# Attention with row maxima formed ahead of the scores: the lead of the maxima cut from four key tiles to two

## The chip, the cores and the metric

The kernel runs on one core of a Trainium2 chip. The metric is the device time of one execution in microseconds (us), the median of several runs. Times inside an execution come from the trace of one profiled execution and count from the start of its span.

## The reference

Inputs are x of shape (2, 2048, 256), three 256x256 projections with biases, and the weights of a gated feed-forward layer. There are 16 heads of width 16, so 32 (batch, head) pairs, called heads 0 to 31 below.

```python
q = hidden_states @ Wq + bq          # k, v alike
q = q * cos_pos + _rotate_half_interleaved(q) * sin_pos   # k alike
scores = jnp.einsum('bhqd,bhkd->bhqk', q, k) / jnp.sqrt(jnp.asarray(HD, hidden_states.dtype))
probs = jax.nn.softmax(scores, axis=-1)
ctx = jnp.einsum('bhqk,bhkd->bhqd', probs, v)
...
x = _layernorm(x + attention(x), axis=-1)
x = _layernorm(x + ffn(x), axis=-1)  # token shift, sigmoid gate, squared relu
```

All of it is float32. The softmax runs over 2048 keys for each of 2048 queries of each head.

## The kernel before

Each head has a period of 16 key tiles (`TILES`). In a tile, PE (TensorE) forms four score matrices of 128 keys x 512 queries (L712), ACT (ScalarE) takes their exponential (L893), and PE multiplies the probabilities of the tile before with the values (L664). A slot is half a tile: two score matmuls and half of such a product. The score matmul has 50 rows: 48 of queries and keys, and two that subtract each query's maximum. So the maxima of a head must stand in its stack of queries (`q_stack`) before its first score.

They are formed ahead by a second stream. A unit is a tile of 128 queries against half of the keys: two matmuls into one of two PSUM tiles `ring_ps` (L645), then one maximum over 128x1024 on DVE (VectorE, L1225). A head has 32 units (`MAX_UNITS`). The maxima matmuls use the half of PE's rows that the scores of the running head leave free. `period_ops(h)` writes the order out by hand: in tile `kt` of head h the units 2*kt + `EARLY` and the one after, of head h+1, or, from 32 on, of head h+2. `EARLY` = 2 * `LEAD`, so with `LEAD` = 4 the last four tiles of a period work on units 0 to 7 of the head after next, which are read from a copy of its stack on the free side (`load_copy`, whose queries reach to `COPY_Q`).

Once unit 31 of head h+1 is read, DVE folds the unit maxima into `neg_max` (L1198, "cut"), POOL (GpSimd) splits it in a high and a low part (`neg_cuts`), DVE turns them (`neg_turned`, L1232, "negs", in tile `NEG_CYCLE`), and SP (SyncE's queue) moves them in two transfers that follow each other:

```python
sp.dma_start(neg_d[h % 2], neg_turned[:, h % 2]).then_inc(neg_out, DMA)      # L461
sp.wait_ge(neg_out, (h + 1) * DMA)
sp.dma_start(dst..., neg_d[h % 2]...).then_inc(neg_in[h % STACKS], DMA)      # L464
```

PE waits for the second at the start of the period, ahead of the first score of the head (`pe.wait_ge(neg_in[...])` in `period`). The last product of the head before stands behind that wait, in tile 0.

Ahead of head 0 there is an opening: 40 units (32 of head 0, eight of head 1) in pairs, behind each pair one or two of 32 projection steps (L609, L622), as `BEHIND_PAIR` says. The transfer for head 0 is asked for behind unit 33 (`OPENING`). In the period of head 30 there is no head after next, so its last four tiles have no units. Head 31's period has none at all, and the feed-forward part follows.

Of the kernel before, what the change touches and what calls it, by code (L numbers as in the profile page):

```python
# [22 lines left out]
BLOCKS = SEQ // TOK  # L23
# [26 lines left out]
PV_CREDIT = 2  # L50
RING_CREDIT = 2
MAX_UNITS = 2 * TILES
LEAD = 4
EARLY = 2 * LEAD
COPY_Q = EARLY // 2 * P
FIRST_COPY = SIDES
TWIN = STACKS - 1
TWIN_FROM = EARLY
NEG_CYCLE = TILES - LEAD
NEG_LOADS = 1  # L60
CTX_BUFS = 2
# [66 lines left out]

OPENING = [("max", 0, u) for u in range(MAX_UNITS)] + [("cut", 0, 0)]
OPENING += [("max", 1, 0), ("max", 1, 1), ("negs", 0, 0)] + [("max", 1, u) for u in range(2, EARLY)]  # L130
BEHIND_PAIR = (2, 1, 2, 1, 2) * ((MAX_UNITS + EARLY) // 10)


def ring_len(ops):
# [29 lines left out]
def build(nc, x_tok, x_blk, w_first, w_qk, b_qk, w_v, b_v, w_rkv, mu, tables, out):  # L164
# [7 lines left out]
    with ExitStack() as ctx:  # L172
# [201 lines left out]
        def stack_rows(h, first, count):  # L374

            side = h % SIDES * SIDE_ROWS
            return slice(side + first, side + first + count)

        def slot_of(h):
            return h // SIDES % (STACKS // SIDES)  # L380
# [199 lines left out]
        def _(pe):  # L580
# [46 lines left out]
            def maximum(k, h, unit):  # L627
# [10 lines left out]
                if (h, unit) == (0, TILES):  # L638
                    pe.wait_ge(late_queries, LATE_QUERIES * DMA)
                if (h, unit) == (0, TWIN_FROM):  # L640
                    pe.wait_ge(twin_in, 3 * PARTS * DMA)
                for c in range(2):
                    if h == 0 and unit >= TWIN_FROM and c:
                        rows, slot = stack_rows(TWIN, 0, ROWS), slot_of(TWIN)
# [110 lines left out]
            for k, op in enumerate(op for op in OPENING if op[0] == "max"):  # L755
                for _ in ring_ops([op], k):
                    pass
                if k % 2:
                    for _ in range(BEHIND_PAIR[k // 2]):
                        project(n)  # L760
# [743 lines left out]
```

## Time and profile before

| | |
|---|---|
| median of 3 runs | 1468.39 us (1467.81 to 1470.98) |
| the profiled execution, its own time | 1470.37 us |
| its span in the trace | 1468.5 us |
| granted clock of PE | 0.999 of full speed |
| busy: PE, DVE, ACT, POOL | 1444.7, 1377.8, 1193.6, 311.5 us |
| first score of heads 16 and 17 | 742.28 and 782.02 us, so a period of 39.75 us |

The execution's own time is 1.9 us over the span, for what lies around it. Busy shares are averages over an opening (to 105 us), 32 periods (to 1385 us) and a last part. What a wait costs is read in its own stretch.

### The profile page before, as it was taken

To read this page: it belongs to the slowest core of one execution; us is meant where nothing else is said; L and a number is where in the kernel's file an instruction comes from. 1 tells how busy PE (TensorE), PEld (TensorE's weight loads), DVE (VectorE), ACT (ScalarE), POOL (GpSimd) and SP (SyncE) were. 2 spreads that over 40 slices of the span, in tenths; PEclk is the share of its full clock that TensorE was granted. 3 is DMA by queue.
4 is the path that set the end of the run, shared out by engine and by line. 5 is a ranking of instruction groups with operands and counts; after the bars stand their busy time and mean duration, and the time that the engine had idled before them with its cause. 6 is when DMAs were issued, how large, how long until landed. Compare 5 with 4: busy or idle time off the path is not lost.

```text
span 1468.5 us, 31675 instructions
## 1 busy us (share of the span) xinstructions
PE 1444.7 (98%) x13108; PEld 604.7 (41%) x13108; DVE 1377.8 (94%) x1457; ACT 1193.6 (81%) x2185; POOL 311.5 (21%) x279
## 2 busy tenths in 40 slices
PE   7999999999999999999999999999999999999998
PEld 6673333333333333333333333333333333333475
DVE  6669999999999999999999999999999999997396
ACT  3338888888888888888888888888888888888745
POOL 5250321032102210032103210241002000001175
PEclk9999999999999999999999999999999999999999
DMA  5845222232223211222223222321112323200153
GB/s 161 241 148 189 41 37 37 37 94 37 37 37 95 36 27 25 79 40 37 36 37 95 37 37 37 95 37 28 23 26 36 51 36 52 37 2 8 24 119 111
DMA packets 72816, 88.20 MB, mean 60 GB/s; under 512 B 48560, under 2 KB 58416, under 8 KB 66464
## 3 DMA queue, kind: packets, MB, share of 16 engines
q1 hardware_dynamic: 72112, 85.39, 27.6%
q8 instruction: 103, 1.69, 0.5%
q10 hardware_dynamic: 560, 0.79, 0.2%
q14 instruction: 41, 0.34, 0.1%
HBM read 29.50 MB, written 14.16 MB: 30 GB/s over the span
## 4 chain that ended last, share of the span: by engine, by line
PE 95%; DVE 2%; ACT 1%; DMA 1%; issue 0%; POOL 0%; POOLq 0%; DVEq 0%
PE pv_ps L664 39%; PE score_ps L712 32%; PE ring_ps L645 15%; PE score_ps L609 2%; PE ring_ps L684 2%; PE score_ps L794 2%; ACT probs L893 1%; PE pv_ps L778 1%; PE score_ps L778 1%; PE pv_ps L609 1%; DVE tile_max L1225 1%; PE score_ps L622 1%; DVE rope L1161 0%; DVE rope L1157 0%; DMA b_qk_s<-b_qk 0%
## 5 line engine op out<-in xcount | busy, mean ns | idle before, releaser
L1225 DVE TENSOR_REDUCE tile_max<-ring_ps 128x1 f32<-128x1024 f32 x1024 | 1232.4, 1217 | 33.7 <-PE ring_ps L645 25.5
L893 ACT ACTIVATE probs<-score_ps 128x512 f32<-128x512 f32 x2048 | 1108.0, 595 | 170.1 <-PE score_ps L712 129.9
L712 PE MATMUL score_ps<-q_stack,k_stack 50*128 50x512 f32 x2048 | 755.0, 448 | 7.1 <-ACT probs L893 6.9
L645 PE MATMUL ring_ps<-k_stack,q_stack 48*128 48x512 f32 x2048 | 736.5, 444 | 0.8 <-DVE tile_max L1225 0.8
L664 PE MATMUL pv_ps<-probs,v_aug 128*32 128x256 f32 x8192 | 649.0, 391 | 0.0
L712 PEld LDWEIGHTS score_ps<-q_stack,k_stack 50*128 50x128 f32 x2048 | 304.4, 185 | 429.1 <-ACT probs L893 412.2
L664 PEld LDWEIGHTS pv_ps<-probs,v_aug 128*32 128x32 f32 x8192 | 165.9, 108 | 367.4 <-issue 190.0
L645 PEld LDWEIGHTS ring_ps<-k_stack,q_stack 48*128 48x128 f32 x2048 | 301.2, 184 | 9.7 <-issue 5.9
L990 POOL TENSOR_TENSOR neg_cuts<-neg_max,zeros 128x16 fp32r<-128x16 f32 x31 | 6.9, 222 | 491.1 <-DVE neg_max L1198 491.1
L982 POOL TENSOR_TENSOR v_aug<-v_all,b_v_s 128x256 f32<-128x256 f32 x32 | 23.7, 741 | 309.6 <-PE pv_ps L664 252.9
L999 POOL TENSOR_TENSOR ctx_part<-ctx_turn,recip 128x256 f32<-128x256 f32 x32 | 20.1, 627 | 266.8 <-DVE recip L1252 266.8
L1011 POOL TENSOR_TENSOR rope<-rope 128x2048 f32<-128x2048 f32 x14 | 63.8, 4572 | 16.7 <-DMA rope<-qk_raw 16.7
L1247 DVE STREAM_TRANSPOSE ctx_turn<-pv_ps 128x512 f32<-128x512 f32 x32 | 22.6, 706 | 21.9 <-PE pv_ps L664 21.9
L1017 POOL TENSOR_TENSOR rope<-rope 128x2048 f32<-128x2048 f32 x7 | 32.1, 4584 | 0.1
L1032 POOL TENSOR_TENSOR rope<-rope 128x2048 fp32r<-128x2048 f32 x7 | 32.0, 4572 | 0.1
L845 ACT ACTIVATE probs<-score_ps,b_qk_s 128x512 f32<-128x512 f32 x21 | 14.2, 688 | 21.9 <-PE score_ps L609 13.7
L684 PE MATMUL ring_ps<-w_rkv_s,rope 128*32 128x256 f32 (+1 forms) x224 | 31.6, 379 | 0.0
L924 ACT ACTIVATE v_all<-score_ps 128x512 f32<-128x512 f32 x14 | 7.6, 594 | 24.6 <-PE score_ps L794 24.6
L684 PEld LDWEIGHTS ring_ps<-w_rkv_s,rope 128*32 128x32 f32 (+1 forms) x224 | 22.5, 144 | 7.3 <-issue 2.4
L794 PE MATMUL score_ps<-rope,w_rkv_s 128*128 128x512 f32 x56 | 25.3, 594 | 0.0
L1327 DVE SCALAR_TENSOR_TENSOR rope<-rope,mu_s 128x512 f32<-128x512 f32 x32 | 22.4, 758 | 2.3 <-ACT rope L905 2.2
L1004 POOL TENSOR_TENSOR z_s<-z_s,ctx_part 128x256 f32<-128x256 f32 x32 | 23.7, 741 | 2.5
(139 smaller groups left out, 550.2 us busy)
## 6 DMA issues: line engine op xcount, KB each, us to landing
k_stack<-rope SPq DMA_DIRECT2D x61, 256.0 KB, 5.0
k_stack<-rope SPq DMA_DIRECT2D x63, 128.0 KB, 4.7
q_stack<-rope SPq DMA_DIRECT2D x31, 256.0 KB, 4.4
qk_raw<-probs SPq DMA_DIRECT2D x28, 256.0 KB, 4.4
rope<-qk_raw SPq DMA_DIRECT2D x7, 1024.0 KB, 4.8
rope<-qk_raw SPq DMA_DIRECT2D x14, 512.0 KB, 6.6
q_stack<-rope SPq DMA_DIRECT2D x33, 128.0 KB, 4.9
z_s<-x_tok SPq DMA_DIRECT2D x2, 2048.0 KB, 11.7
```

Of the source, the lines that this page charges most:

```text
L609: mm = pe.matmul(bank, w[:, c, :], x[:, c, :], start=term == 0 and c == 0, stop=term == 2 and c == CHUNKS - 1)
L645: mm = pe.matmul(ring_ps[k % 2][:, c * TOK:(c + 1) * TOK], q_stack[rows, slot, qt * P:(qt + 1) * P], k_stack[rows, slot, lo + c * TOK:lo + ...
L664: mm = pe.matmul(pv_ps[j * VCOLS:(j + 1) * VCOLS, t], v_aug[:, h % 2, kt, :], probs[:, kt % 2, j, t], start=kt == 0 and half == 0, stop=kt ...
L684: mm = pe.matmul(r_ps[n][g:g + width, q * DIM:(q + 1) * DIM], mixed[:, n % MIXED_BUFS, 0, c, q * P + g:q * P + g + width], w_rkv_s[:, 0, c ...
L712: mm = pe.matmul(score_ps[n % SCORE_BANKS][:, :], k_stack[rows, slot, kt * P:(kt + 1) * P], queries[:, j], start=True, stop=True)
L778: mm = pe.matmul(value_ps[q // 2][:, q % 2 * DIM:(q % 2 + 1) * DIM], key_act[:, n % 2, c, q * P:(q + 1) * P], w_rkv_s[:, 2, c, :], start=c ...
L794: mm = pe.matmul(o, w_rkv_s[:, 1, c, m * P:(m + 1) * P], mixed[:, n % MIXED_BUFS, 1, c, :], start=c == 0, stop=c == CHUNKS - 1)
L893: act.activation(probs[:, kt % 2, j, :], score_ps[n % SCORE_BANKS][:, :], ACT.Exp, scale=SCALE).then_inc(exps_done, 1)
L1011: pool.tensor_tensor(blocks, blocks, tables_s[:, :, w, :], ALU.mult).then_inc(quad_step, 1)
L1017: pool.tensor_tensor(raw, raw, swapped, ALU.add).then_inc(quad_step, 1)
L1032: pool.tensor_tensor(cuts[:, g % 2, 1, :].bitcast(F32R), raw, cuts[:, g % 2, 0, :], ALU.subtract)\
L1225: dve.reduce_max(tile_max[:, h % 2, unit // 2, unit % 2:unit % 2 + 1], slot[:, :], AX.X)\
```

## The change

`LEAD` goes from 4 to 2, and with it `EARLY` from 8 to 4. The order of a period moves: units 4 to 31 of head h+1 fill tiles 0 to 13, and units 0 to 3 of head h+2 the last two tiles. `cut` moves from the end of tile 11 to the end of tile 13, and `negs` from tile 12 to tile 14 (`NEG_CYCLE` = `TILES` - `LEAD`). The copy of a stack holds 256 queries in place of 512 (`COPY_Q`). `TWIN_FROM` keeps its value of 8. The opening has 36 units, and `BEHIND_PAIR` spreads the same 32 projection steps behind 18 pairs in place of 20. The last four units of head 31, which stood in tiles 10 and 11 of head 30's period, stand in its tiles 12 and 13, and the four fewer of the opening are made up there.

```diff
-LEAD = 4
+LEAD = 2
 EARLY = 2 * LEAD
 COPY_Q = EARLY // 2 * P
 FIRST_COPY = SIDES
 TWIN = STACKS - 1
-TWIN_FROM = EARLY
+TWIN_FROM = BLOCKS * 2
 NEG_CYCLE = TILES - LEAD
...
-BEHIND_PAIR = (2, 1, 2, 1, 2) * ((MAX_UNITS + EARLY) // 10)
+BEHIND_PAIR = (2, 1, 2, 2, 2) * 3 + (2, 2, 1)
```

DVE's order in a period, from the maxima ahead of the fold to the reciprocal of the next period (L1247 turns the product of the finished head in tile 0), before:

```order
L1225 TENSOR_REDUCE tile_max<-ring_ps 128x1 x14
L1198 TENSOR_REDUCE neg_max<-tile_max 128x16
L1225 TENSOR_REDUCE tile_max<-ring_ps 128x1
L1232 STREAM_TRANSPOSE neg_turned<-neg_cuts 128x32
L1225 TENSOR_REDUCE tile_max<-ring_ps 128x1 x8
L1247 STREAM_TRANSPOSE ctx_turn<-pv_ps 128x512
```

And now:

```order
L1225 TENSOR_REDUCE tile_max<-ring_ps 128x1 x18
L1198 TENSOR_REDUCE neg_max<-tile_max 128x16
L1225 TENSOR_REDUCE tile_max<-ring_ps 128x1
L1232 STREAM_TRANSPOSE neg_turned<-neg_cuts 128x32
L1225 TENSOR_REDUCE tile_max<-ring_ps 128x1 x4
L1247 STREAM_TRANSPOSE ctx_turn<-pv_ps 128x512
```

The fold and the turn stand four maxima later; between the turn and the next period's L1247 stand four maxima in place of eight. PE's order at the end of the opening, from its last pair of units to the first score of head 0, before:

```order
L645 MATMUL ring_ps<-k_stack,q_stack 128x512 x4
L622 MATMUL score_ps<-w_high,x_split 128x256 x4
L622 MATMUL score_ps<-w_low,x_split 128x256 x2
L622 MATMUL score_ps<-w_high,x_split 128x256 x4
L622 MATMUL score_ps<-w_low,x_split 128x256 x2
L622 MATMUL score_ps<-w_high,x_split 128x256 x4
L622 MATMUL score_ps<-w_low,x_split 128x256 x2
L622 MATMUL score_ps<-w_high,x_split 128x256 x4
L622 MATMUL score_ps<-w_low,x_split 128x256 x2
L712 MATMUL score_ps<-q_stack,k_stack 128x512
```

And now:

```order
L645 MATMUL ring_ps<-k_stack,q_stack 128x512 x4
L622 MATMUL score_ps<-w_high,x_split 128x256 x4
L622 MATMUL score_ps<-w_low,x_split 128x256 x2
L622 MATMUL score_ps<-w_high,x_split 128x256 x4
L622 MATMUL score_ps<-w_low,x_split 128x256 x2
L712 MATMUL score_ps<-q_stack,k_stack 128x512
```

One projection step stands behind the last pair in place of two, and that pair is now units 34 and 35, not 38 and 39. The orders of ACT and POOL are the same as before, and SP's differs in the size of the copies alone.

## Rows read from the trace of the kernel before

**Rows 1.** Busy time by stretch: from:to, length, engines' busy us, clock, DMA share, GB/s.

```profile
600.00:1000.00 400.00, 397.85 (x3866) 149.49 (x3864) 397.04 (x373) 348.33 (x644) 87.00 (x70) 1.00 0.26 50
```

**Rows 2.** The page, section 5: busy, mean ns | idle before, releaser.

```profile
L1225 DVE TENSOR_REDUCE tile_max<-ring_ps 128x1 f32<-128x1024 f32 x1024 | 1232.4, 1217 | 33.7 <-PE ring_ps L645 25.5
...
L645 PE MATMUL ring_ps<-k_stack,q_stack 48*128 48x512 f32 x2048 | 736.5, 444 | 0.8 <-DVE tile_max L1225 0.8
```

**Rows 3.** Timeline of PE around the start of head 16: start, length, what.

```profile
734.86 0.50 PE L712 MATMUL score_ps<-q_stack,k_stack 50*128 50x512 f32 x1
...
739.80 0.50 PE L712 MATMUL score_ps<-q_stack,k_stack 50*128 50x512 f32 x1
...
741.71 0.64 PE L664 MATMUL pv_ps<-probs,v_aug 128*32 128x256 f32 x8
742.28 0.50 PE L712 MATMUL score_ps<-q_stack,k_stack 50*128 50x512 f32 x1
```

**Rows 4.** Timeline of DVE in the same stretch.

```profile
733.21 0.19 DVE L1198 TENSOR_REDUCE neg_max<-tile_max 128x16 f32<-128x32 f32 x1
...
734.45 0.20 DVE L1232 STREAM_TRANSPOSE neg_turned<-neg_cuts 128x32 f32<-128x32 f32 x1
734.57 9.74 DVE L1225 TENSOR_REDUCE tile_max<-ring_ps 128x1 f32<-128x1024 f32 x8
```

**Rows 5.** Timeline of SP's DMA issues in the same stretch.

```profile
734.68 0.32 SPq L461 DMA_DIRECT2D neg_turned_rows<-neg_turned  x1
736.09 0.67 SPq L464 DMA_DIRECT2D q_stack<-neg_turned_rows  x1
```

**Rows 6.** Busy time by stretch, same place, for its DMA share.

```profile
735.60:735.80 0.20, 0.20 (x8) 0.08 (x8) 0.20 (x2) 0.20 (x1) 0.00 (x0) 1.00 0.22 32
...
738.00:738.20 0.20, 0.20 (x6) 0.15 (x8) 0.19 (x2) 0.20 (x1) 0.00 (x0) 1.00 0.14 21
738.20:738.40 0.20, 0.20 (x8) 0.00 (x0) 0.20 (x1) 0.20 (x1) 0.00 (x0) 1.00 0.00 0
```

**Rows 7.** The same view ahead of head 4.

```profile
261.20:261.40 0.20, 0.20 (x8) 0.00 (x0) 0.20 (x1) 0.20 (x2) 0.00 (x0) 1.00 0.01 1
261.40:261.60 0.20, 0.20 (x6) 0.18 (x4) 0.20 (x1) 0.20 (x1) 0.00 (x0) 1.00 0.00 0
```

**Rows 8.** Timeline of PE at the first score of head 4.

```profile
265.14 0.50 PE L712 MATMUL score_ps<-q_stack,k_stack 50*128 50x512 f32 x1
```

**Rows 9.** Waits of SP's queue: line, releaser: us in total, times, longest.

```profile
SPq L464 <- DMA neg_turned_rows<-neg_turned: 43.0, 32, 3.1
```

**Rows 10.** Timeline of PE in head 30's last tiles, without maxima.

```profile
1336.18 0.74 PE L712 MATMUL score_ps<-q_stack,k_stack 50*128 50x512 f32 x2
...
1337.41 0.73 PE L712 MATMUL score_ps<-q_stack,k_stack 50*128 50x512 f32 x2
```

**Rows 11.** Timeline of PE at the end of the opening.

```profile
101.04 1.20 PE L645 MATMUL ring_ps<-k_stack,q_stack 48*128 48x512 f32 x4
102.17 0.74 PE L622 MATMUL score_ps<-w_high,x_split 128*128 128x256 f32 x4
...
105.46 0.47 PE L712 MATMUL score_ps<-q_stack,k_stack 50*128 50x512 f32 x1 [0.20 <-ACTq L881]
```

**Rows 12.** Timeline of DVE at the end of the opening.

```profile
95.95 0.21 DVE L1232 STREAM_TRANSPOSE neg_turned<-neg_cuts 128x32 f32<-128x32 f32 x1 [1.39 <-POOL neg_cuts L992]
...
99.08 2.35 DVE L1225 TENSOR_REDUCE tile_max<-ring_ps 128x1 f32<-128x1024 f32 x2 [0.68 <-PE ring_ps L645]
```

**Rows 13.** Timeline of SP at the end of the opening.

```profile
98.27 0.76 SPq L464 DMA_DIRECT2D q_stack<-neg_turned_rows  x1
```

**Rows 14.** Busy time by stretch at the end of the execution.

```profile
1461.00:1463.00 2.00, 1.31 (x7) 0.80 (x5) 1.90 (x8) 1.36 (x3) 1.61 (x3) 1.00 0.00 0
1463.00:1465.00 2.00, 0.00 (x0) 0.00 (x0) 1.85 (x8) 0.89 (x2) 1.70 (x4) 1.00 0.79 262
1465.00:1468.50 3.50, 0.00 (x0) 0.00 (x0) 0.64 (x2) 0.20 (x1) 0.45 (x1) 0.55 0.45 150
```

## The prediction

> **What bounds the kernel now.** I read first a long stretch of the periods by engine. In the 400 us from 600 to 1000, PE is busy 397.85 us and DVE 397.04 us, at full clock [rows 1]: both stand within 1% of full. The idle times say which of them leads. DVE idled 33.7 us in the whole execution, most of it for PE's maxima matmuls, while those matmuls waited 0.8 us for DVE [rows 2]. So PE sets the pace and DVE runs right behind it. PE's timeline shows the pace: scores start at 734.86 and at 739.80, four slots apart [rows 3], 4.94 us or 1.235 us a slot. Thirty-two slots make 39.5 us of a period of 39.75 us. At the end of head 30, where no maxima are formed, a slot takes 1337.41 - 1336.18 = 1.23 us [rows 10], the same: the maxima matmuls cost PE no time beside the scores. What matters for the change is then the one thing that PE needs at a head's start and that it does not need to wait for today: the negated maxima.
>
> **The way of the negated maxima today.** For head 16, DVE folds at 733.21 and turns from 734.45 to 734.65 [rows 4]; SP stores at 734.68 and starts the reload at 736.09 [rows 5], 1.41 us later. The store's last packets fall before 735.8 [rows 6], some 0.4 us ahead of the issue that waits for them, which I take as the time from the last packet to the semaphore. The reload has no recorded landing, but the DMA share shows it: packets until 738.2, none after [rows 6]. With 0.4 us more it lands at 738.6, that is 2.5 us after its issue and 3.95 us after the turn. PE's first score of head 16 starts at 742.28 [rows 3]. The slack is 3.68 us. For head 4 the last packets fall right behind 261.2 [rows 7], the landing is at 261.6, the first score at 265.14 [rows 8]: 3.54 us of slack.
>
> **The change part by part.**
>
> *Fold and turn four units later.* DVE takes one unit for each slot of PE, with no backlog (the idle times above), so four units are four slots: 4.94 us [rows 3]. POOL's cut stands between fold and turn, and its distance to both is unchanged. Everything behind the turn moves with it: two transfers, and SP has nothing else to issue between them. PE's need does not move. The wait at the head's start is 4.94 - 3.68 = 1.26 us by head 16 and 4.94 - 3.54 = 1.40 us by head 4. I take the mean, 1.33 us, for 31 heads (1 to 31): 41.2 us.
>
> *Slower stores.* SP waited 43.0 us in 32 times for the store, up to 3.1 us [rows 9]. Head 16's wait was 736.09 - 735.00 = 1.09 us [rows 5], and 32 of these are 34.9 us. So 8.1 us lie over that, in a few heads. In the opening it was 98.27 - 96.51 less 1.09 = 0.67 us (the turn ends at 96.16 [rows 12], and the store is issued for 0.32 us right behind it). The other 7.4 us come straight on PE's waits: every head waits now, so no slack takes them up. + 7.4 us.
>
> *Starting again.* A score overlaps the end of the product ahead of it by 0.07 us (741.71 + 0.64 against 742.28 [rows 3]). After a wait it does not: 31 x 0.07 = 2.2 us. Nothing is won back behind the wait: the last product of the head before stands behind it in PE's order, so the period's first tile runs as today, late as a whole. ACT and DVE only idle: both take their work from PE.
>
> *The opening.* Four units fewer. Two units take PE 102.17 - 101.04 = 1.13 us [rows 11], and there nothing runs beside them, so PE would come to the first score 2.26 us earlier, at 103.2. But head 0's transfer is asked for behind unit 33, and behind that unit's pair stand now three projection steps and one pair instead of six and three. A step takes (105.3 - 102.17) / 2 = 1.56 us, with 105.3 for the end of the last (the score at 105.46 idled 0.2 before it [rows 11]). Unit pair 32 and 33 then starts 3 x 1.56 + 1.13 + 1.13 = 6.9 us ahead of 103.2, at 96.3. DVE is done with a pair 99.08 + 2.35 - 98.3 = 3.1 us after PE begins it (PE begins that pair one step and one pair ahead of 101.04, at 98.3 [rows 11, 12]), so at 99.4; the turn adds 0.2. The two transfers took 98.27 - 96.16 = 2.1 us to the reload's issue [rows 12, 13], and 2.5 us more as above: the first score can start at 104.2 in place of 105.46. The opening gives 1.2 us. Its bounds are 2.3 us (no wait) and nothing.
>
> *At no cost.* The four units that the opening gives up end in tiles 12 and 13 of head 30, where a slot lasts as long with them as without. The smaller copies leave SP and the DMAs less to do. The loads of the stacks keep their places and have most of a period. In head 30 DVE's first work for the feed-forward part moves 5 us back behind the turn; it serves head 31's later tiles, and PE comes to these later too.
>
> The sum: 41.2 + 7.4 + 2.2 - 1.2 = 49.6 us. On the profiled execution's 1470.37 us this gives 1520.0 us, on its span 1518.1 us. That execution lies 2 us over the median of the runs, so the time I predict for the median is 1468.39 + 49.6 = **1518.0 us**.
>
> *The bounds.* The reload's time is the one unseen price. From below, it could take what the store takes from issue to landing, 1.41 us, and 0.35 us more for its longer issue (0.67 against 0.32 [rows 5]): 1.76 in place of 2.5 us. That is 0.74 us less a head, 23 us in all, 1495 us. From above, every store could wait 43.0 / 32 = 1.34 us and some heads up to 3.1 us; if all took 0.7 us more than head 16's, as the worst heads do in part, that would be 22 us less the 7.4 counted: 1533 us.
>
> **The rivals.**
>
> *The wait brings PE's clock down.* At the end of the execution PE stops at 1462.3, keeps the full clock to 1465, and shows 0.55 of it after [rows 14]. So some 3 us of idling are followed by the half clock. The waits that I expect are 1.3 us in most heads, and near 3 us in one or two. If the clock fell at each head and stayed at half for a few slots, each such slot would take up to 1.23 us more; two of them a head are 31 x 2.46 = 76 us more, about 1594 us. It decides from waits near 3 us on. Against it: 1.3 us stays well under the one pause for which a row shows a fall. I give it 4 in 100. The Trainium skill ("TensorE: Matmul & The Clock Gate", "HAM oscillation — how this bites in real kernels") tells of a matmul loop that pauses for a DMA at each step and starts cold every time. By that rule the half clock would come back at each head; whether a pause of 1.3 us is enough, no row here shows.
>
> *The stores are slow everywhere.* Something at tiles 14 and 15 makes both transfers longer, such as the slow stores of some heads [rows 9]. Then 0.7 to 1 us more a head: 1535 to 1545 us. For it: it happens in some heads, for a reason that I cannot read. Against it: the DMA share is close to nothing around these transfers [rows 6, 7] and stays so two tiles later, since SP issues the next loads only after a head's last score. 9 in 100.
>
> *The transfers are hidden (no slower).* The turn would end at 734.65 + 4.94 = 739.6, 2.69 us ahead of the first score. If both transfers landed within these 2.69 us, no head would wait, and the opening alone would count: 1468.39 - 2.3 = 1466.1 us. That is the point from which it decides. Against it stand the 3.95 us above, and the store alone, which takes 1.44 us of them from the turn to the reload's issue; the reload would have to land 1.25 us after its issue, and its packets still flow 1.9 us after it [rows 6]. 3 in 100.
>
> **How the numbers follow.** My forecast has 84 in 100, the clock 4, slow stores 9, the hidden transfers 3. The range from 1495 to 1540 us takes in the bounds of the reload and most of the slow stores. A difference under 0.2% (3 us) is what a measurement of this kernel can't tell from no change. The forecast and two of the rivals lie far over it; the third lies within it, 2 us faster. So slower 0.96, same 0.03, faster 0.01.
>
> **What the profile after would show.** Right: a period of about 41.1 us in place of 39.75; PE's first score of each head idle ahead of it for 1.2 to 1.5 us, with the reload's DMA as the releaser, and about 3 us at the worst head; DVE's idle time up by some 45 us, ACT's too; slots inside a period still 1.235 us; first score of head 0 near 104.2; clock at 1.00 in every period. Wrong: slots longer right behind a wait (the clock), reloads issued 2 us behind the turn in all heads (slow stores), or first scores with no idle time (hidden). The prediction falls most easily with the reload's landing, which I read from packets and an added 0.4 us.

## The result

The changed kernel takes 1563.99 us (median of 4 runs, 1553.87 to 1594.11), the kernel before 1468.45 us (1467.81 to 1470.98): a ratio of 1.0624, 95% interval 1.0581 to 1.0667. That is slower, as forecast, but by 95.5 us in place of 49.6, and above the range of 1495 to 1540 us. Times scatter over 40 us where before they lay within 3. Ratios, here and in the table below, leave out runs that lie over 1.5% above the fastest of their kernel (here the one of 1594.11 us), so they can be lower than the quotient of the medians. The profiled execution is the longest of them (span 1592.3 us), so its rows are read for the mechanism, and the sizes are set against all runs.

The page of the kernel after: busy time, the clock granted to PE in 40 slices of the span (tenths; 9 is 90% or more), and the two groups that answer to [rows 2] and to the scores.

```profile
PE 1522.9 (96%) x13108; PEld 625.7 (39%) x13108; DVE 1378.8 (87%) x1457; ACT 1193.6 (75%) x2185; POOL 311.6 (20%) x279
...
PEclk9999999968978667699999999999999999999999
...
L1225 DVE TENSOR_REDUCE tile_max<-ring_ps 128x1 f32<-128x1024 f32 x1024 | 1235.4, 1218 | 154.2 <-PE ring_ps L645 147.2
...
L712 PE MATMUL score_ps<-q_stack,k_stack 50*128 50x512 f32 x2048 | 795.2, 470 | 52.6 <-DMA q_stack<-neg_turned_rows 46.4
```

The clock stood at 9 in every slice before:

```profile
PEclk9999999999999999999999999999999999999999
```

It falls here in eight slices, all in the first half. DVE's idle time before its maxima grew from 33.7 to 154.2 us, by 120 us in place of the 45 us foreseen, and the scores idle 46.4 us for the reload of the negated maxima, which did not show before. The waits of PE name it too (us in total, times, longest):

```profile
PE score_ps L712 <- DMA q_stack<-neg_turned_rows: 46.4, 31, 3.1
```

For an ordinary head, 16, the timelines of DVE, SP and PE answer to [rows 3] to [rows 5]:

```profile
839.83 0.20 DVE L1232 STREAM_TRANSPOSE neg_turned<-neg_cuts 128x32 f32<-128x32 f32 x1
...
844.83 1.23 DVE L1225 TENSOR_REDUCE tile_max<-ring_ps 128x1 f32<-128x1024 f32 x1 [1.32 <-PE ring_ps L645]
```

```profile
840.05 0.32 SPq L461 DMA_DIRECT2D neg_turned_rows<-neg_turned  x1
841.46 0.67 SPq L464 DMA_DIRECT2D q_stack<-neg_turned_rows  x1
```

```profile
842.14 0.64 PE L664 MATMUL pv_ps<-probs,v_aug 128*32 128x256 f32 x8
843.99 0.50 PE L712 MATMUL score_ps<-q_stack,k_stack 50*128 50x512 f32 x1 [1.21 <-DMA q_stack<-neg_turned_rows]
```

The turn ends at 840.03, the reload is issued at 841.46, and PE idles 1.21 us from the end of the product to the first score. This is the prediction's step, to 0.1 us. DVE idles as long. The first score of head 0 starts at 102.40, where the prediction had 104.2. Here is head 5, with a slow store (SP, then PE):

```profile
307.75 0.32 SPq L461 DMA_DIRECT2D neg_turned_rows<-neg_turned  x1
310.76 0.66 SPq L464 DMA_DIRECT2D q_stack<-neg_turned_rows  x1
```

```profile
309.83 0.64 PE L664 MATMUL pv_ps<-probs,v_aug 128*32 128x256 f32 x8
313.54 0.77 PE L712 MATMUL score_ps<-q_stack,k_stack 50*128 50x512 f32 x1 [3.07 <-DMA q_stack<-neg_turned_rows]
```

The store took 3.01 us to the reload's issue, PE idled 3.07 us, and its first score took 0.77 us in place of 0.50. Busy time by period, from head 4 to head 8 and for head 16 (from:to, length, PE, PEld, DVE, ACT, POOL, granted clock, DMA share, GB/s):

```profile
270.50:313.50 43.00, 39.73 (x384) 14.95 (x384) 39.47 (x36) 34.53 (x64) 2.55 (x5) 1.00 0.21 34
313.50:369.80 56.30, 54.18 (x384) 18.84 (x384) 39.97 (x36) 34.65 (x64) 11.54 (x7) 0.70 0.23 58
369.80:417.20 47.40, 45.35 (x384) 16.48 (x384) 39.73 (x36) 34.65 (x64) 8.93 (x7) 0.86 0.18 28
417.20:458.90 41.70, 39.69 (x385) 14.89 (x385) 39.47 (x36) 34.65 (x64) 7.08 (x6) 1.00 0.20 32
458.90:512.30 53.40, 51.19 (x384) 17.97 (x385) 39.96 (x36) 34.64 (x64) 2.53 (x5) 0.74 0.16 25
844.00:885.20 41.20, 39.69 (x385) 14.91 (x385) 39.46 (x36) 34.64 (x64) 2.55 (x5) 1.00 0.22 34
```

The same 384 matmuls take 56.3 us with a mean clock of 0.70 in head 5 and 41.2 us at full clock in head 16.

### The profile page after: what moved, and what is told of

The parts are those of the page before. It is cut to its first block, busy times and chain, and to the rows that moved or that the text cites. A ratio compares the mean times of both kernels' runs of the same rounds, so it can differ in the third digit from the quotient of the medians.

```text
span 1592.3 us, 31675 instructions
## 1 busy us (share of the span) xinstructions
PE 1522.9 (96%) x13108; PEld 625.7 (39%) x13108; DVE 1378.8 (87%) x1457; ACT 1193.6 (75%) x2185; POOL 311.6 (20%) x279
## 4 chain that ended last, share of the span: by engine, by line
DVE 55%; PE 30%; DMA 9%; issue 4%; ACT 0%; POOL 0%; POOLq 0%; DVEq 0%; ACTq 0%
DVE tile_max L1225 53%; PE score_ps L712 11%; PE pv_ps L664 9%; DMA q_stack<-neg_turned_rows 5%; DMA neg_turned_rows<-neg_turned 3%; PE ring_ps L645 2%; PE score_ps L609 2%; PE ring_ps L684 2%; PE score_ps L794 2%; DVE ctx_turn L1247 1%; PE pv_ps L778 1%; PE score_ps L778 1%; DMA qk_raw<-probs 1%; PE pv_ps L609 0%; DVE neg_turned L1232 0%
## 5 line engine op out<-in xcount | busy, mean ns | idle before, releaser
L1225 DVE TENSOR_REDUCE tile_max<-ring_ps 128x1 f32<-128x1024 f32 x1024 | 1235.4, 1218 | 154.2 <-PE ring_ps L645 147.2
L712 PE MATMUL score_ps<-q_stack,k_stack 50*128 50x512 f32 x2048 | 795.2, 470 | 52.6 <-DMA q_stack<-neg_turned_rows 46.4
L645 PE MATMUL ring_ps<-k_stack,q_stack 48*128 48x512 f32 x2048 | 776.2, 465 | 0.4 <-DVE tile_max L1225 0.4
L664 PE MATMUL pv_ps<-probs,v_aug 128*32 128x256 f32 x8192 | 685.9, 411 | 0.0
L712 PEld LDWEIGHTS score_ps<-q_stack,k_stack 50*128 50x128 f32 x2048 | 322.2, 195 | 510.8 <-ACT probs L893 440.2
L664 PEld LDWEIGHTS pv_ps<-probs,v_aug 128*32 128x32 f32 x8192 | 169.8, 110 | 390.3 <-issue 238.5
L645 PEld LDWEIGHTS ring_ps<-k_stack,q_stack 48*128 48x128 f32 x2048 | 318.7, 195 | 7.6 <-issue 5.5
L1247 DVE STREAM_TRANSPOSE ctx_turn<-pv_ps 128x512 f32<-128x512 f32 x32 | 22.7, 709 | 21.6 <-PE pv_ps L664 21.6
```

The costliest lines, as they stand in the source:

```text
L645: mm = pe.matmul(ring_ps[k % 2][:, c * TOK:(c + 1) * TOK], q_stack[rows, slot, qt * P:(qt + 1) * P], k_stack[rows, slot, lo + c * TOK:lo + ...
L664: mm = pe.matmul(pv_ps[j * VCOLS:(j + 1) * VCOLS, t], v_aug[:, h % 2, kt, :], probs[:, kt % 2, j, t], start=kt == 0 and half == 0, stop=kt ...
L712: mm = pe.matmul(score_ps[n % SCORE_BANKS][:, :], k_stack[rows, slot, kt * P:(kt + 1) * P], queries[:, j], start=True, stop=True)
L1225: dve.reduce_max(tile_max[:, h % 2, unit // 2, unit % 2:unit % 2 + 1], slot[:, :], AX.X)\
L1247: dve.transpose(ctx_turn[:, h % CTX_BUFS].rearrange("p c v -> p (c v)"), pv_ps[:, :]).then_inc(pv_turned, 1)
```

## The experiments

Times are medians of all runs. Each ratio is taken against runs of the kernel before that were measured beside them. The mean clock is that of each run, lowest to highest.

| kernel | us | ratio, 95% interval | mean clock |
|---|---|---|---|
| after, first runs | 1563.99 | 1.0624 (1.0581 to 1.0667) | 0.941 to 0.970 |
| after_again | 1573.63 | 1.0621 (1.0579 to 1.0662) | 0.949 to 0.970 |
| no_wait | 1466.52 | 0.9984 (0.9974 to 0.9993) | 0.999 to 1.000 |
| turn_14 | 1548.32 | 1.0535 (1.0494 to 1.0576) | 0.969 to 0.980 |
| turn_15 | 1739.11 | 1.1783 (1.1704 to 1.1861) | 0.870 to 0.904 |
| fillers | 1539.88 | 1.0489 (1.0458 to 1.0520) | 0.980 to 0.992 |
| fillers_12 | 1559.14 | 1.0619 (1.0587 to 1.0651) | 0.990 to 0.999 |
| pv_first | 1593.63 | 1.0721 (1.0632 to 1.0811) | 0.930 to 0.962 |
| one_hop | 1477.60 | 1.0059 (1.0044 to 1.0074) | 0.999 in the profile |
| lead_3 | 1471.84 | 1.0009 (0.9999 to 1.0019) | 0.999 to 1.000 |
| spread, spread_2, spread_3 | 1469.76, 1469.54, 1469.89 | 1.0003, 0.9994, 0.9998 (each within 0.001) | 0.999 to 1.000 in the profiles |
| spread_4 | 1608.34 | 1.0934 (1.0911 to 1.0958) | 0.999 in the profile |

**The wait taken away.** The score matmul uses `ROWS` in place of `ROWS_M`, and PE's wait goes:

```diff
-                pe.wait_ge(neg_in[h % STACKS], neg_loaded(h))
...
-                        rows, slot = stack_rows(h, 0, ROWS_M), slot_of(h)
+                        rows, slot = stack_rows(h, 0, ROWS), slot_of(h)
```

Not shown are a wait that SP gets for the reload of the head before, and one that PE gets at the end of the last period. They keep the transfers in order.

> The changed kernel, but the scores use the 48 rows without the two that subtract the maxima, so the subtraction is left out and PE no longer waits for the reload; the transfers, the fold and the turn still take place in tiles 13 and 14. Theory (the wait at each head's start, and half clock after it): no idle time at a head's first score, clock 1.00 in every period, about 1466 to 1469 us. Rival (the new order or the shorter lead costs time or clock by itself, in the slots): it stays over 1500 us with periods over 40 us. Rival (the half clock comes from outside the program): stretches of half clock here too.

As the theory said: full clock, and 2.4 us faster than before (1.0 to 3.8 us by the interval). The new order and the shorter lead cost nothing, and the gain agrees with the 2.26 us worked out for the opening's four units fewer. It is not shown that it comes from there: with the old opening, head 0's first score starts anywhere from 103.60 (turn_14) to 107.48 us (spread_3), and here at 103.68. The loss hangs on the wait.

**The wait alone, in the old order.** `NEG_CYCLE = TILES - 2`, then `TILES - 1`, in the kernel before.

> The kernel of before, with its lead of four tiles and its opening, and only the turn of the negated maxima put off from tile 12 to tile 14. Theory (wait and half clock): the same waits as in the changed kernel, 1.2 to 1.3 us for each of 31 heads and up to 3 us where a store is slow, 45 to 50 us in all, and stretches of half clock that cost 0.42 us for each us of them: 1515 us at the least, 1550 to 1600 us as measured. Rival (the shorter lead itself, the copies or the opening): near 1468 us.

```profile
PE score_ps L712 <- DMA q_stack<-neg_turned_rows: 42.2, 30, 2.6
```

42.2 us of waits and stretches of half clock, 1548.3 us. That is over the 1515 us at the least and 2 us under the 1550 to 1600 us expected. Moving the turn alone gives most of the loss. Its waits are 0.1 us shorter than the changed kernel's: the turn ends 2.87 us before PE is done with the head before, and 2.75 us there, where DVE folds just ahead of it.

> The kernel of before, with only the turn of the negated maxima put off from tile 12 to tile 15: a wait of 1.2 + 2.47 = 3.7 us at each head's start. Theory (waits as time, and half clock behind long waits at 0.42 us for each us of it): 31 x 3.7 = 115 us of waits, so 1583 us without any half clock; with a fall at nearly every head, of 3 to 40 us each, 1650 to 1950 us and a mean clock under 0.9. Rival (half clock follows the slow stores themselves or an outside cause, not the length of the wait): a fall in some ten heads as before, 1600 to 1640 us.

```profile
PE score_ps L712 <- DMA q_stack<-neg_turned_rows: 108.5, 30, 4.3
```

And its clock in 40 slices of the span:

```profile
PEclk9996998798969786766869899899899889989999
```

The waits were 3.5 to 3.7 us in nearly all heads, 108.5 us in sum, and each of heads 1 to 30 has a stretch of half clock that begins between 2.2 us before its first score and 1.1 us behind it. The stores of these heads were fast (1.41 to 1.47 us to the reload's issue), so half clock does not need a slow store. What its heads have in common is the long wait.

**The changed kernel once more.**

> The changed kernel once more, unchanged, for a second profile beside the others. Theory (half clock follows long waits, and the long waits come from slow stores that fall on other heads each time): waits of 1.2 to 1.3 us at most heads, half clock behind the waits near 2 us and over, at other heads than in the first profile, 1550 to 1590 us. Rival (slow stores and half clock belong to places of the program): slow stores again at heads 3 and 5 to 11, and half clock behind the same heads.

Its clock in 40 slices of the span:

```profile
PEclk9998899996895897899999999999999999999999
```

The slow stores (head 0 left aside) fell on heads 1 and 4 to 11 this time, and on 3 and 5 to 11 in the first profile. Five heads (5, 6, 8, 9 and 11) have half clock in both. So the theory's "at other heads" failed in the main, and that the slow stores belong to places of the program is not refuted: the kernel before has them at heads 25 to 31, and the runs below with its order of work at 25 to 31 (spread), 23 and 25 to 31 (spread_2) and 23 to 31 (spread_3). Small changes move them: turn_14 has them at 1 to 7 and 31, no_wait at 1, 2 and 6 to 13, lead_3 at 11 and 15 to 20, fillers at 2, 3, 18 and 19, and turn_15 at 31 alone. Most come in episodes of some 200 to 350 us. That half clock needs no slow store rests on turn_15, and not on this run.

**PE kept busy ahead of the wait.**

PE repeats head h's first score matmul (with 48 rows), six times and then twelve (`FILLERS`).

```diff
+                if h > 0:
...
+                    pe.wait_ge(exps_done, n + 1)
+                    for _ in range(FILLERS):
+                        pe.matmul(score_ps[n % SCORE_BANKS][:, :], k_stack[rows, slot, 0:P], queries[:, 0], start=True, stop=True)
                 pe.wait_ge(neg_in[h % STACKS], neg_loaded(h))
```

> The changed kernel, where PE repeats a score matmul six times (some 1.3 us, into the bank that the first score overwrites) ahead of its wait for the reload, so that it does not idle there in most heads. Theory (idling brings the clock down): the waits remain as time, 45 to 55 us, but the clock stays at 1.00 except perhaps after slow stores (3 us): 1513 to 1525 us. Rival (the half clock has another cause, such as the program's order or an outside one): stretches of half clock as before, 1550 to 1590 us.

PE's scores and the repeated matmuls (busy us, mean ns, idle before them):

```profile
L720 PE MATMUL score_ps<-q_stack,k_stack 50*128 50x512 f32 x2048 | 757.2, 450 | 11.7 <-ACT probs L901 6.4 <-DMA q_stack<-neg_turned_rows 5.4
...
L706 PE MATMUL score_ps<-q_stack,k_stack 48*128 48x512 f32 x186 | 52.2, 413 | 0.0
```

The waits stayed as time, but the waits that PE saw fell to 5.4 us. The median clock of the runs is 0.984, against 0.956 in after_again, which was measured beside it, and the ratio is 1.0489 against 1.0621, some 19 us less. The clock did not come back to full, so 1539.9 us is above what I expected. In the profile, six matmuls leave 1.36 us of idling at head 2 and 1.08 us at head 18, both with slow stores, and beside them stand half clock of 17.1 and 3.4 us.

> The changed kernel with twelve repeated score matmuls (2.6 us) ahead of the wait in each head in place of six. They are longer than most waits, so they cost time themselves: 1466.5 + 31 x 2.7 = 1550 us. Theory (only PE's idling brings the clock down): even behind a slow store under 0.7 us of idling is left, so the clock is 0.999 in every run and the times agree within 0.3%, 1545 to 1556 us. Rival (a stop of the real work is enough, or the cause is outside): stretches of half clock remain and times scatter over 15 us or more.

```profile
PEclk9999999999999999999999999999999999999999
```

Three of four runs lie at 0.997 to 0.999 and within 3 us, the fourth at 0.990 and 1567.7 us. That is near the expectation and not in it: the median is 3 us over the band, and the clock was to be 0.999 in each. The fillers cost 2.85 us a head (a period of 42.60 us against 39.75), twice the ordinary wait, and the time can't be told from the changed kernel's (1.0619 against 1.0621 and 1.0624): what the longer stop of the real work costs, the clock gives back. In the profile two stretches of 3.4 us at half clock are left, and PE shows no idle time ahead of them or in them. Here is the one at head 3, the stretch ahead of it and the half clock:

```profile
229.00:232.40 3.40, 3.40 (x20) 2.52 (x16) 0.86 (x1) 0.45 (x1) 0.00 (x0) 1.00 0.75 92
232.40:235.80 3.40, 3.40 (x24) 1.42 (x22) 1.94 (x2) 1.54 (x3) 1.10 (x2) 0.50 0.80 140
```

So score matmuls on PE during the wait hold the clock nearly always, and idle time that the trace shows is not the whole cause.

**Real work in the wait.** The last product of the head before (`pv(h - 1, TILES - 1)`) moves ahead of the wait.

> The changed kernel, but the last product of the head before (1.0 us of PE) stands ahead of the wait for the reload in place of behind the first two scores. PE then idles about 0.45 us for the last exponential, works for 1.0 us, and the reload has landed. Theory (idling of PE in one piece brings the clock down; the end of the wait is what counts for ACT): the head's start comes 1.2 to 1.5 us late all the same, since ACT, busy 96% of a slot, starts again no earlier, so the waits still cost 35 to 48 us; the pieces of idling are short except behind slow stores, so there is little half clock: 1505 to 1535 us. Rival (the position of the product is free time): 1480 to 1490 us.

PE's timeline from the end of head 13 to the start of head 14, whose store was fast, and the clock in 40 slices:

```profile
755.75 0.40 PE L714 MATMUL score_ps<-q_stack,k_stack 50*128 50x512 f32 x1
756.07 2.06 PE L664 MATMUL pv_ps<-probs,v_aug 128*32 128x256 f32 x24
758.09 0.50 PE L714 MATMUL score_ps<-q_stack,k_stack 50*128 50x512 f32 x1
```

```profile
PEclk9999878877799897889999998999989999999999
```

The first half held: a period without half clock is 41.1 us, as in the changed kernel. The second failed. PE shows 24 product matmuls in a row and no idle time of its own, but the clock still fell in heads with fast stores (12, 19, 24), there 4.5 to 4.6 us behind the first score, and is no better overall, 0.930 to 0.962. The busy time of that row is modelled and holds the wait for the last exponential, which ACT ends at 757.03. The product did not hold the clock where the score matmuls did; what sets them apart I leave open.

**One transfer in place of two.** SP issues the reload right behind the store, from the buffer of the head before (so the subtraction uses another head's maxima). Not shown are two waits of SP ahead of the store, for the transfers of the head before.

```diff
-                sp.wait_ge(neg_out, (h + 1) * DMA)
+                if h == 0:
+                    sp.wait_ge(neg_out, DMA)
...
-                             neg_d[h % 2].rearrange(...)
+                             neg_d[(h - 1) % 2 if h > 0 else 0].rearrange(...)
```

> The changed kernel, but the reload doesn't wait for the store: it brings the maxima that were stored for the head before, so the subtraction uses another head's maxima. PE waits for it as ever. Theory (the wait is the sum of two transfers, 1.44 us to the store's landing and 2.5 us for the reload, less 2.7 us): the reload alone lands 2.5 to 2.9 us behind the turn, a wait of 0 to 0.3 us per head, no slow stores in the way, clock 0.999: 1466 to 1476 us. Rival (the reload is slow in itself at this place, or whatever stands at a head's start costs the time): over 1500 us.

```profile
741.36 0.32 SPq L464 DMA_DIRECT2D neg_turned_rows<-neg_turned  x1
741.73 0.66 SPq L468 DMA_DIRECT2D q_stack<-neg_turned_rows  x1
```

```profile
743.44 0.64 PE L669 MATMUL pv_ps<-probs,v_aug 128*32 128x256 f32 x8
744.31 0.50 PE L717 MATMUL score_ps<-q_stack,k_stack 50*128 50x512 f32 x1 [0.23 <-DMA q_stack<-neg_turned_rows]
```

The reload goes out 0.37 us behind the store and PE idles 0.23 us. 1477.6 us is 1.6 us over the expected band: a period lasts 40.1 us, 0.35 us over 39.75, which is 10.5 us in the 30 heads that wait. The clock is full. From the reload's issue to the first score pass 2.4 to 2.8 us, as in the changed kernel where stores are fast, so the prediction's 2.5 us for the reload holds, and what is gone is the wait for the store.

**A lead of three tiles.** `LEAD = 3` with `BEHIND_PAIR = (2, 1, 2, 2, 1) * 3 + (2, 2, 2, 2)`.

> A lead of three tiles: fold at the end of tile 12, turn in tile 13, six early units, 38 units in the opening. Theory (what counts is whether both transfers land before the head's first score, and 3.7 us of slack less 2.47 us leaves 1.2 us): no wait in most heads, 0 to 0.9 us where a store is slow, full clock, 1.1 us less in the opening: 1466 to 1471 us. Rival (each tile less of lead costs its share): half way to the changed kernel, 1500 to 1520 us.

```profile
600.00:1000.00 400.00, 397.59 (x3864) 149.42 (x3856) 396.69 (x372) 347.87 (x644) 86.94 (x70) 1.00 0.25 49
```

The stretch reads as [rows 1]. In the profile, the slow stores of heads 11 and 15 bring two waits of 0.49 and 0.26 us; else there is none. The cost has a threshold at the slack, and is not shared out by tile. The time can't be told from the kernel before; it lies 0.8 us over the expected band, and the opening's 1.1 us does not show in it. No version that computes the reference came out faster than the kernel before.

**The same loss without a pause.** A small write on DVE behind each maximum, in the kernel before, to make DVE the bound in every slot.

```diff
                             .then_inc(ring_freed, 1)
+                        if h > 1:
+                            after(dve, spare_set, spared[0] - 1)
+                            dve.memset(spare[:, spared[0] % 2, :], 0.0).then_inc(spare_set, 1)
+                            spared[0] += 1
```

> The kernel of before, with a small extra write on DVE behind each maximum of heads 2 to 31 (960 in all, 0.06 to 0.08 us each by the like of it in the trace of before). DVE then needs 1.29 us for a unit and becomes the bound, so PE idles about as much in a period as in the changed kernel (1.3 to 2.2 us), but a little in each slot, with no pause at a head's start. Theory (it is the pause in one piece that brings the clock down): clock 0.999 in every run, periods of 41.2 to 42 us, 1515 to 1535 us with a scatter of 3 us. Rival (PE's lower share of work is enough): stretches of half clock, scatter over 10 us, 1550 us and more.

> As the run with one extra write behind each maximum, which filled DVE's slot exactly (1.18 us of a maximum and 0.06 us of the write in a slot of 1.235 us) and cost nothing; now two writes (1,920 in all). DVE then needs 1.30 us for a unit, and PE idles about 0.06 us in each slot, 2 to 3 us in a period, in small pieces: 1468.5 + 960 x 0.065 = 1531 us, and up to 1558 us if DVE's other work in a period (0.9 us) comes on the path too. Theory (the clock falls behind a pause in one piece): clock 0.999 in every run, scatter under 4 us. Rival (a lower share of work is enough): stretches of half clock, mean clock under 0.99 and a scatter over 10 us.

> As the two runs with small extra writes behind each maximum, which DVE took in between for nothing; now one write of 96 elements a row. By the write of 256 elements in the trace of before (0.27 us) and those of 4 (0.06 us) it takes 0.14 us, so a unit takes DVE 1.18 + 0.14 = 1.32 us against PE's slot of 1.235 us: 960 x 0.085 = 82 us more, and up to 27 us for DVE's other work: 1550 to 1580 us. PE idles 2.6 to 3.5 us in a period, twice what it does in the changed kernel, in pieces of about 0.1 us. Theory (the clock falls behind a pause in one piece): clock 0.999 in every run, scatter under 5 us. Rival (a lower share of work is enough): mean clock under 0.98, stretches of half clock and a scatter over 10 us.

All three expectations failed: not one added time. DVE's timeline with the first write (4 elements), and with the third (96) where DVE is behind:

```profile
700.76 0.06 DVE L1232 MEMSET spare<- 128x4 f32 x1
700.82 1.23 DVE L1228 TENSOR_REDUCE tile_max<-ring_ps 128x1 f32<-128x1024 f32 x1
702.00 0.06 DVE L1232 MEMSET spare<- 128x4 f32 x1
702.06 1.23 DVE L1228 TENSOR_REDUCE tile_max<-ring_ps 128x1 f32<-128x1024 f32 x1
```

```profile
708.35 1.16 DVE L1228 TENSOR_REDUCE tile_max<-ring_ps 128x1 f32<-128x1024 f32 x1
709.48 0.14 DVE L1232 MEMSET spare<- 128x96 f32 x1
709.54 1.16 DVE L1228 TENSOR_REDUCE tile_max<-ring_ps 128x1 f32<-128x1024 f32 x1
```

In a slot where DVE waits for PE's next unit, a maximum shows 1.23 us; where it is behind, 1.16 us, and the write overlaps it. DVE had 0.05 to 0.1 us a unit to spare. These three say nothing on the clock.

> The extra write behind each maximum now has 256 elements a row, 0.27 us by the trace of before. In the run with 96 elements a backlog was worked off at 1.185 us for a maximum and its write of 0.14 us, so this needs 1.185 + 0.13 = 1.315 us against PE's slot of 1.235 us: 960 x 0.08 = 77 us more and up to 27 us for DVE's other work, 1545 to 1575 us. PE idles 2.5 to 3.4 us in a period, more than in the changed kernel, in pieces of about 0.1 us. Theory (the clock falls behind a pause in one piece): clock 0.999 in every run, scatter under 5 us. Rival (a lower share of work is enough): mean clock under 0.98 and a scatter over 10 us.

DVE's and PE's timelines with 256 elements:

```profile
700.83 1.16 DVE L1228 TENSOR_REDUCE tile_max<-ring_ps 128x1 f32<-128x1024 f32 x1
701.99 0.27 DVE L1232 MEMSET spare<- 128x256 f32 x1
702.18 1.16 DVE L1228 TENSOR_REDUCE tile_max<-ring_ps 128x1 f32<-128x1024 f32 x1
```

```profile
700.56 0.50 PE L715 MATMUL score_ps<-q_stack,k_stack 50*128 50x512 f32 x1
...
701.91 0.50 PE L715 MATMUL score_ps<-q_stack,k_stack 50*128 50x512 f32 x1
```

A slot is now 1.35 us, 9% over 1.235, and a period of heads 1 to 29 is 44.2 to 45.2 us. The time is 33 us over what I expected, as the write costs 0.12 us a unit and not 0.08. The clock is 0.999 and the four times lie within 2.7 us. From 600 to 1000 us PE does 3472 matmuls, 10% fewer than the 3866 of [rows 1]:

```profile
600.00:1000.00 400.00, 397.93 (x3472) 169.77 (x3469) 399.14 (x621) 312.85 (x579) 62.78 (x55) 1.00 0.22 41
```

PE's row still shows it busy for 397.93 us, so the waiting does not show in it as idle time. The changed kernel loses its clock beside pauses of 1.6 to 3.3 us in one piece, 4 to 8% of a period. So a lower share of work, evenly spread, is not enough.

## Why the prediction was wrong

**The waits: right.** I had 41.2 us for ordinary waits, 7.4 for slow stores and 2.2 for starting again, 50.8 us. The profiled waits are 46.4 us by the row above and 49.4 us in after_again; with the 0.07 us of lost overlap for 31 heads, 48.6 and 51.6. An ordinary period is 41.1 to 41.2 us, as predicted. The opening gained 2.4 us by no_wait (1.0 to 3.8) where I took 1.2, and there the kernel has no wait.

**The clock: the step that failed.** The sum has no term for the clock: it takes every slot at full speed, "clock at 1.00 in every period". The reason stands in the rival "The wait brings PE's clock down", at 4 in 100: "1.3 us stays well under the one pause for which a row shows a fall". A pause of 3 us at the end of the execution shows that 3 us are followed by half clock, not that less are safe. And the sum itself had longer waits: I took slow stores as extra time, and said "near 3 us in one or two" heads, while the three profiles of after, after_again and turn_14 have eight, nine and seven heads with a wait of 1.6 us or more. In these three, the clock's record shows a stretch of half clock beside 18 of the 24 waits of 1.6 us or more, 3.4 to 41 us long and 22.6 us on average; of 68 shorter waits (0.8 to 1.6 us) five, 3.4 us each. The Trainium skill ("TensorE: Matmul & The Clock Gate", "HAM oscillation — how this bites in real kernels") tells of a loop that pauses for a DMA at each step and starts cold every time. Here that came at every head in turn_15, and in the changed kernel at some heads only.

**When the clock falls, and for how long.** In these three profiles and that of turn_15 there are 53 stretches of half clock around a head's start. The 22 that begin 0.2 to 1.0 us behind the head's first score all last 3.4 us. The 31 that begin earlier, from 2.2 us before the first score on, or later, up to 1.8 us behind it, last 6.8 to 44.4 us. So the length goes with the moment of the fall and not with that of the wait, which in turn_15 is 3.5 to 3.7 us before stretches of 3.4 and of 44.4 us. Why it does is not shown.

**What the half clock costs.** Head 5's period is 56.27 us with 34.1 us of half clock by the clock's record: less 39.75 and the 2.09 us that head 6 waits, 14.4 / 34.1 = 0.42 us for each us; heads 6 and 8 to 11 give 0.41 to 0.42. Taking 2 x (1 - mean clock) x span as each run's time at half clock and 0.42 us for each, an estimate, the eight runs of the changed kernel come down from spans of 1552 to 1592 us to 1510 to 1518 us. The forecast's span, 1518.1 us, is 1516.9 with the opening at 2.4 us. So the other 39 to 78 us are half clock. That the rival's 76 us lies among them is luck: it stood for two slots at each of 31 heads, and what came were eight and ten stretches, the long ones all in heads 1 to 11.

**The rivals.** Hidden transfers are out, by the row of waits. Slow stores everywhere did not come: most come in episodes, and their sum was the same as before (43.1 us of SP's waits in 32, against 43.0 [rows 9]):

```profile
SPq L464 <- DMA neg_turned_rows<-neg_turned: 43.1, 32, 2.9
```

What is open: why stores are slow in episodes and what puts these early or late, why the product matmuls don't hold the clock, why some pauses bring half clock and others don't, and why the moment of the fall goes with its length.

## What to carry to other kernels

A wait on the engine that sets the pace costs more than its length when the engine idles in one piece: here 1.2 us a head, and up to 3.3 us at some, were some 50 us as time and 39 to 78 us more as half clock. Size the slack of a prefetch by the slowest landing that the trace shows (here 2 us over the ordinary one) and not by the usual one; three tiles of lead were free, two were not. And a busy share near 100% on an engine that follows another can hold waiting: put a small operation beside it to see.

## What the hardware showed

With a pause of PE of 1.6 to 3.3 us, once in a period of some 41 us, half clock began within 2 us of the pause's end in 18 of 24 cases. With one of 3.5 to 4.3 us it began in 30 of 30, from 2.2 us before the pause's end to 1.1 us behind it. PE then stayed at 1.2 GHz for up to 41 us in the first and 44 us in the second, although from its first score on it did not idle in that time. The store of 16 KB took 1.41 us to the next issue in most heads, and 1.9 to 3.7 us in episodes. DVE's maximum over 128x1024 shows 1.22 us on average when DVE keeps pace with PE, and 1.16 us when it is behind.
